# A two-layer graph network on one core: in the second layer GpSimd's gathers wait for TensorE's work of five groups back instead of three

## What is computed

```python
# layer 0
m = relu(x[src]) + 1e-7
a = softmax of m over the edges of one dst, per feature
x = layernorm(x + (x + segment_sum(a * m, dst)) @ W + b)
# layer 1
Q, K, V = x @ Wq + bq, x @ Wk + bk, x @ Wv + bv        # 12,500 x 8 x 12
E = edge_attr @ We + be                                # 212,500 x 8 x 12
score = exp(clip((K[src] * Q[dst] / sqrt(12) * E).sum(-1), -5, 5))
wV = segment_sum(V[src] * score, dst);  Z = segment_sum(score, dst)
x = layernorm(x + wV / (Z + 1e-6))
```

## Time and the profile before

| | |
|---|---|
| median of 3 runs | 4892.83 us (4892.27 to 4892.83) |
| profiled execution | span of 4892.4 us from its first instruction to its last |
| PE, DVE, ACT, POOL busy | 63%, 47%, 18%, 64% of the span |
| first layer's gathers | from 2.9 us to 2384.5 us |
| second layer's gathers | from 2404.9 us to 4878.6 us |
| DMA | 78 GB/s over the span |

### The profile page before, as it was taken

One profiled execution on the slowest core, in us unless ns is written; L12 is line 12 of the kernel. 1 busy time (PEld: TensorE's weight loads), 2 busy tenths in 40 slices (PEclk: granted clock), 3 DMA queues, 4 the chain that ended last, 5 costly groups with the idle time before them and its releaser, 6 DMA issues.

```text
span 4892.4 us, 43885 instructions
## 1 busy us (share of the span) xinstructions
PE 3098.1 (63%) x13152; PEld 2767.9 (57%) x13152; DVE 2300.2 (47%) x5605; ACT 870.5 (18%) x1966; POOL 3143.9 (64%) x3330
## 2 busy tenths in 40 slices
PE   3445444555555455455578777878777877877777
PEld 3344434444444444444477677767677777767676
DVE  5434344334433443344445555555555555555555
ACT  1222222222222222222201111111111111111111
POOL 6666666666666666666566666666666666666665
PEclk8666666666656667656665655565666565566665
DMA  3111111121111111111244444444444444444443
GB/s 97 40 40 43 42 39 40 40 45 40 40 44 41 39 40 45 40 39 40 67 111 111 114 112 114 112 111 117 112 111 111 114 112 114 112 114 110 115 113 98
DMA packets 290371, 383.51 MB, mean 78 GB/s; under 512 B 154382, under 2 KB 196911, under 8 KB 290127
## 3 DMA queue, kind: packets, MB, share of 16 engines
q0 software_dynamic: 132864, 251.83, 21.4%
q1 hardware_dynamic: 157263, 128.81, 9.5%
HBM read 360.62 MB, written 19.72 MB: 78 GB/s over the span
## 4 chain that ended last, share of the span: by engine, by line
POOL 31%; issue 23%; PE 18%; another core or an unknown queue 15%; DVE 9%; DMA 2%; ACT 2%; DVEq 0%; SPq 0%; ACTq 0%
POOL rows L454 31%; PE banks L605 4%; PE banks L586 4%; PE banks L577 4%; PE banks L547 3%; DVE onehot L817 2%; PE banks L596 2%; DMA rows<-in_x,src_i 1%; DVE sums L942 1%; DVE ex L930 1%; DMA rows<-key_value,src_i 1%; DVE banks L850 1%; ACT onehot_t L717 1%; DVE sums L940 1%
## 5 line engine op out<-in xcount | busy, mean ns | idle before, releaser
L454 POOL DMA_INDIRECT rows<-key_value,src_i x1661 | 1571.9, 946 | 922.2 <-issue 431.8
L454 POOL DMA_INDIRECT rows<-in_x,src_i x1661 | 1570.6, 946 | 811.6 <-issue 469.1
L547 PE MATMUL banks<-ex,onehot 128*128 128x192 f32 x3322 | 1036.0, 483 | 1026.7 <-DVE ex L930 810.5
L547 PEld LDWEIGHTS banks<-ex,onehot 128*128 128x128 f32 x3322 | 865.2, 288 | 1188.8 <-DVE ex L930 933.9
L586 PE MATMUL banks<-qw,onehot_t 128*128 128x192 f32 x1664 | 609.2, 515 | 401.2 <-ACT onehot_t L717 233.1
L605 PEld LDWEIGHTS banks<-onehot,vals 128*104 128x104 f32 x3322 | 601.2, 272 | 260.2 <-issue 210.3
L605 PE MATMUL banks<-onehot,vals 128*104 128x64 f32 x3322 | 608.2, 359 | 183.8 <-issue 151.5
L586 PEld LDWEIGHTS banks<-qw,onehot_t 128*128 128x128 f32 x1664 | 440.3, 302 | 449.1 <-ACT onehot_t L717 258.4
L577 PE MATMUL banks<-we_sb,ea 97*128 97x96 f32 x3322 | 672.1, 372 | 0.0
L577 PEld LDWEIGHTS banks<-we_sb,ea 97*128 97x128 f32 x3322 | 662.2, 295 | 0.0
L930 DVE SCALAR_TENSOR_TENSOR ex<-banks,ex 128x384 f32<-128x384 f32 x416 | 229.0, 550 | 795.7 <-issue 654.5
(11 more groups left out here) (107 smaller groups left out, 1480.4 us busy)
## 6 DMA issues: line engine op xcount, KB each, us to landing
ea<-in_edge_t SPq DMA_DIRECT2D x415, 192.0 KB
rows<-in_x,src_i POOLq DMA_INDIRECT x1661
rows<-key_value,src_i POOLq DMA_INDIRECT x1661
qw<-query SPq DMA_DIRECT2D x832, 24.0 KB
key_value<-qkv SPq DMA_DIRECT2D x24, 400.0 KB
x<-in_x SPq DMA_DIRECT2D x7, 672.0 KB, 8.2
query<-qkv SPq DMA_DIRECT2D x24, 192.0 KB
out<-outs SPq DMA_DIRECT2D x24, 192.0 KB
```

The lines of the kernel that those rows point to most:

```text
L454: pool.indirect_dma_start(out=to[0:n, r, u, :], out_offset=None, in_=table, in_offset=bass.IndirectOffsetOnAxis(ap=src_i[0:n, g * G + u:g ...
L547: last = nc.tensor.matmul(ps_sum0[b], onehot[:, r, u, :], ex[:, b, u, :], start=u == 0, stop=u == n - 1)
```

## The change

One constant, `PACE1 = 5`, takes the place of `PACE` in POOL's loop of the second layer. The first five groups are gathered without a wait. After that the four gathers of group g wait for `sum_values(g - 5)`, `turn_onehot(g - 3)`, `edge_products(g - 3)` and `query_rows(g - 3)`. Nothing else differs: no instruction of another engine, no buffer and no transfer is added or taken away.

```diff
 PACE = 3
+PACE1 = 5
...
                 for g in range(NG):
-                    if g < PACE:
+                    if g < PACE1:
                         gather(g, g % R1, rows, key_value, s_row1[g % R1])
                     else:
-                        pool.wait_ge(s_sum1, g - PACE + 1)
+                        pool.wait_ge(s_sum1, g - PACE1 + 1)
                         gather_tile(g, 0, g % R1, rows, key_value, s_row1[g % R1])
-                        marks = ((s_tr1, g - PACE + 3), (s_ee, g - PACE + 3), (s_qe, g - PACE + 3))
+                        marks = ((s_tr1, g - PACE1 + 3), (s_ee, g - PACE1 + 3), (s_qe, g - PACE1 + 3))
                         for u in range(1, tiles_of_group(g)):
                             s_mark, n_done = marks[u - 1]
                             pool.wait_ge(s_mark, n_done)
                             gather_tile(g, u, g % R1, rows, key_value, s_row1[g % R1])
```

## The result

The changed kernel takes 4903.21 us (median of 15 runs, 4898.10 to 4907.93), the kernel before 4892.27 us (15 runs, 4889.77 to 4895.22) on the same chip. The ratio is 1.0021, with a 95% interval from 1.0014 to 1.0028: 10.9 us slower, between 7 and 14. The profiled execution has a span of 4902.1 us.

The account below looks back on a forecast made before the run. The prediction took the second layer to be bound by its gathers, about 1.45 us each, with PE's signals held up during bursts. Start +10.8, middle 0 and end -1.3 us gave +9.5, so 4902 us; 8-in-10 range 4872 to 4920 us.

Parts of the forecast that it names:

- The bound: Second layer: each gather costs about 1.45 us of an unnamed resource, against 1.25 us on POOL; 1661 take 2375 to 2490 us.
- Signals held to the end of the burst: Second layer: PE's signals are held up while a burst of gathers is worked off, then let through together; 6.3 us once.
- 5 to 6 us behind its turn in every second group: Sign in the changed second layer: ACT's one-hot copy (line 717) still starts this late after PE's turn, between bursts of eight.
- Middle, 0 us: Middle of the second layer: POOL stops at the same PE signals as before, so no change; bounds 0 and -154 us.
- the prediction's two signs of being wrong: Middle of the second layer: bursts of 12 or 16 common, or restarts less than 1.45 us per gather apart.
- Start, +10.8 us: Start of the second layer: a first burst of 20 gathers, 28.60 us against 17.76, delays all work; bounds 10.0 and 12.0.
- End, -1.3 us: End of the second layer: two last groups run without gathers beside them, saving one late signal; bounds 0 and -5.9 us.
- The sum: Whole kernel: start and end terms give +9.5 us, so 4902 us, 0.19% above the median; chance 0.52.
- the same: Whole kernel: a time within 0.2% (9.8 us) of before, between 4883.0 and 4902.6 us; chance 0.50.
- Longer bursts making the layer faster: Rival, second layer: POOL stops less often, pace 5.73 us for a group, 95 us less, 4798 us; chance 0.08.
- Rows earlier: Rival, second layer: DVE's waits for gathered rows shrink, up to 154 us; a quarter gives 4854 us; chance 0.08.
- Slower at every chunk: Rival, second layer: longer backlogs cost 1.5 us more at each of some 24 node chunks, 4938 us; chance 0.08.

Follow-up runs that it names:

- one_gather: Kernel before, but from group 6 on only the first tile's rows of each second-layer group are gathered: 3933.1 us, ratio 0.809 to before's 4856.9 us.
- half_rows: Kernel before, but from group 6 on each second-layer gather takes 64 rows in place of 128: 4855.1 us, ratio 0.9995 to before's 4858.1 us.
- middle_lead5_b: Kernel before, with a lead of five only for groups 200 to 299 of the second layer: 4898.2 us, ratio 1.0013 to before's 4892.3 us.
- three_gathers: Kernel before, but from group 6 on three of a second-layer group's four tiles are gathered: 4333.9 us, ratio 0.892 to before's 4858.1 us.
- late_lead5_b: Kernel before, with a lead of five from group 200 of the second layer on: 4901.8 us, ratio 1.0022 to before's 4892.3 us.

## Why the prediction was right, and where it wasn't

*The bound* was read rightly in that the gathers hold the signals up and set the pace: one_gather takes the late signals away together with the gathers, and half_rows shows that their number counts and not their rows. The step from there to a resource that takes "about 1.45 us" for each gather isn't borne out. Restarts come 17.76, 22.64, 28.41 and 33.23 us after the start of bursts of 12, 16, 20 and 24 gathers. Less 1.25 us for each gather, that leaves 2.8, 2.6, 3.4 and 3.2 us, and 2.0 us for the steady bursts of eight. (middle_lead5_b's 16 leave 1.3, with two more short stops close behind them.) So a burst costs GpSimd's issuing and one stop of about 2 to 3 us, and 1.48 us is the average over short bursts; at 24 it is 1.38. The resting DMA engines and the 1.28 us of three_gathers point the same way. The forecast wasn't hurt, since it took the burst of 20 as a whole from the earlier trace rows. What holds the signals is still not named by any record. It is also a thing of the chip: on another, 1.25 us of GpSimd is the bound and signals come at once. The prediction had no words for that.

*Signals held to the end of the burst* is right for the long bursts and too strong for the others. The 6.3 us of the earlier trace rows is the longest of the 416 in the trace before. 178 of its copies wait for a "remote" release; they start 1.5 to 6.3 us after their turn's recorded end, 2.9 us in the median, and only 96 of them start within 0.6 us of a restart of GpSimd. In the changed kernel it is 186 copies and 2.6 us, and behind the first burst only seven over 5 us. So the sign "5 to 6 us behind its turn in every second group" did not come. No term of the sum used it.

*Middle, 0 us.* The changed kernel's middle was 4.7 us faster in its one trace (1.4868 against 1.4897 us for a gather over 1640 steps and 1648); one pair of traces doesn't tell that from chance. The larger lead's gain of up to 154 us did not come: DVE's waits for rows went, and its idle time before `weigh_values` grew. The bursts stayed at eight, with none of 12 or 16 in the middle, and one of 176 came under 1.45 us for a gather, so neither of the prediction's two signs of being wrong came. middle_lead5_b agrees within its interval: the rise and the fall explain its time without a term for the hundred groups between them.

*Start, +10.8 us.* Measured +10.65 (28.41 - 17.76), 1.33 us for each of the eight gathers. The step behind it, that all work is later by as much because signals wait until the burst is over, is shown by the copy's 20.02 us. Where the prediction tied this to the start it was too narrow: late_lead5_b pays the same 10.6 us at group 200.

*End, -1.3 us.* 25.9 us behind the last gather (23 to 26 forecast), last gather at 4876.24 (within 2 us of 4878 forecast). The stretch behind it grew by 11.2 us against the 11.9 us of the 8 gathers saved, so -0.7 us.

*The sum*, +9.5, stands against +10.9 (7 to 14) in the runs, but in the pair of traces only +5.2 us lie in the second layer and 4.5 us ahead of it. That part is open. The three other traces of kernels that differ only in the second layer, on a chip with the same time of before, have their first gather at 2403.4 to 2404.9 us as before, so the 4.5 us look like one execution's chance. The three traces on the chip of 4858 us have it at 2386.7, 2388.6 and 2390.7 us, so such differences do occur. But then the layer's own share should be larger on average than in the one trace, and I have only single traces. In those of late_lead5_b and middle_lead5_b the second layer is longer by 7.7 and 8.0 us, at medians of +9.5 and +5.9. That the forecast of 4902 met 4903.2 so closely is therefore in part luck: the long burst and the end bear its terms out, the sum is only borne out to some 5 us. The measured time lies 0.6 us above the 4902.6 us up to which the prediction spoke of no change, on the side to which it gave 0.34, while it gave 0.50 to "the same".

*The rivals.* Longer bursts making the layer faster: refuted by four kernels with more lead, none of them faster on any chip. Rows earlier: refuted, since that wait went without a gain. Slower at every chunk: the +36 us did not come. The rule of the Trainium skill that each increment of a semaphore by a matmul adds about 26 ns ("TensorE: Matmul & The Clock Gate", "The cost: per-tile semaphore tail") fits the chip of 4194 us, with 0.04 us from turn to copy, and one_gather; it doesn't fit during bursts of gathers on the slower chips, where the runs show up to 17.3 us in the changed kernel.

No kernel here that gathers all its rows beats the one before. On the slower chips a lead of two is too short, and leads of five and six cost about 5 us for each group over three, once, of which a part comes back; a lead of four was measured only on the chip of 4194 us, where it changes nothing.

## What to carry to other kernels

If an engine that issues DMAs stops and restarts in step with several unrelated waiters, measure the time from restart to restart for bursts of several lengths, and not for one: here it is 12.0 us for 8 and 33.2 us for 24, which splits into 1.25 us for each gather and one stop of about 2 to 3 us. One period out of 200 can mislead, as the 6.3 us did; ask for the median. Choose the least lead that keeps such a queue from running empty, and take the price of a deeper one as (extra entries) x (time of one, here 1.3 us), paid once at each rise of the lead and not in each burst. And before a reading is generalised, run the same kernel on another chip: 700 us of this kernel's 4893 depend on it.

## What of the hardware was unexpected

- The same program takes 4892, 4857 or 4194 us, according to the chip (each seen at one time only). Within a chip the runs agree to 0.3%. The difference to 4194 us is nearly all in the stops between gathers, 307 us up to the start of the second layer (first gather of the second at 2404.94 against 2098.3 us) and 396 us in the second.
- On the slower chips the second layer takes 1.48 us for a gather on average, with 128 rows and with 64 (half_rows), and on all chips GpSimd issues a gather of 128 rows in 1.25 us.
- On the slower chips, during bursts of gathers, TensorE's recorded ends and what waits for them are up to 6.3 us apart in the kernel before, 14.2 us in a burst of 16 and 17.3 us in one of 20; with one gather for a group the same waits end at once. That it is the signal that is late, and not work that was recorded too early, can be read from the earlier trace rows: the eight edge products stand behind the turn on TensorE and take it 0.97 us, and yet SP's load, which waits for them, starts 0.08 us after ACT's copy, which waits for the turn. Late work would have kept them about 1 us apart.
